# Soft-MoE and random-feature attention over 16 batch rows: paired clips and exponentials, a copy moved to ScalarE, two contexts moved to another PSUM bank

## The reference, cut to what matters

```python
qkv = x @ Wqkv + bqkv                        # 16 heads of 8
xn = x / norm(x)                             # q and k, per head
proj = einsum('bhtd,rhdm->rbhtm', xn, omega) # R = 2 nodes, M = 32 features
feat = exp(clip(proj * sqrt(2 s) - s, -20, 20)) * const
# causal linear attention: ctx = qf . cumsum(kf x v), den = qf . cumsum(kf)
out_ch = ctx / maximum(den, 1e-6)
...
logits = einsum('bsd,etd->bset', xn, se)     # 512 slots
dispatch = softmax(logits, axis=experts); slots = dispatch^T xn
h = gelu(slots @ w1); processed = h @ w2     # hidden 512
out = softmax(logits, over all slots) @ processed
```

## Time and profile before

| | |
|---|---|
| median of 3 runs | 474.83 (474.27 to 476.93) |
| the profiled execution | 474.87, its span 473.1 |
| mean granted TensorE clock | 0.977 |
| one inner row, from `shift` to `shift` | 27.04 and 27.18 in turn |
| busy: PE / DVE / ACT / POOL | 435.3 / 376.0 / 314.4 / 186.7 |
| clips (L747) / exponentials (L533), 128 each | 98.8 / 87.8 |
| the stack's copy (L794) x15 | 13.8 |

### The profile page before, as it was taken

The page is one execution under the profiler, slowest core; times in us unless marked ns, Lnnn a source line. Parts: engine busy times, 40 slices in busy tenths (PEclk is TensorE's granted clock), DMA queues, the critical chain, the costliest instruction groups (busy, mean ns, idle before and its releaser), DMA issues.

```text
span 473.1 us, 16005 instructions
## 1 busy us (share of the span) xinstructions
PE 435.3 (92%) x5712; PEld 359.2 (76%) x5712; DVE 376.0 (79%) x956; ACT 314.4 (66%) x577; POOL 186.7 (39%) x276
## 2 busy tenths in 40 slices
PE   3087999999999999999999999999999999999993
PEld 2056888888787888788887888878788887888782
DVE  5579788887988888887988889788898879677462
ACT  4226768676758667686766768675767767676761
POOL 4303444443533343353334345353334435334220
PEclk9589999999999999999999999999999999999998
DMA  2430202020020202011020202002020201102000
GB/s 54 99 65 1 46 13 48 24 46 21 12 51 11 53 13 44 24 32 24 11 55 11 44 22 44 17 6 55 11 50 17 44 11 24 34 2 58 1 13 12
DMA packets 45779, 14.46 MB, mean 31 GB/s; under 512 B 35640, under 2 KB 45624, under 8 KB 45752
## 3 DMA queue, kind: packets, MB, share of 16 engines
q1 hardware_dynamic: 45176, 13.77, 13.9%
q10 hardware_dynamic: 576, 0.33, 0.2%
HBM read 3.61 MB, written 2.10 MB: 12 GB/s over the span
## 4 chain that ended last, share of the span: by engine, by line
PE 68%; DVE 21%; issue 5%; SPq 2%; ACT 2%; DMA 1%; DVEq 1%
PE x L952 11%; PE p_s L1003 8%; PE x L1160 7%; PE x L1172 6%; PE p_t L1003 6%; DVE arg L747 6%; PE p_s L1015 5%; PE x L1151 4%; PE x L1015 3%; PE x L1094 3%; DVE slot_v L802 3%; PE p_s L988 2%; PE x L1129 2%; DVE s_sb L753 2%; PE x L1105 2%
## 5 line engine op out<-in xcount | busy, mean ns | idle before, releaser
L464 POOL TENSOR_TENSOR s_sb<-s_sb,causal 128x256 f32<-128x256 f32 x96 | 68.6, 734 | 112.3 <-ACT s_sb L538 110.3
L533 ACT ACTIVATE feat<-arg,f_bias 128x512 f32<-128x512 f32 x128 | 87.8, 717 | 0.2
L747 DVE TENSOR_SCALAR arg<-p_s,f_low,f_high 128x512 f32<-128x512 f32 x64 | 48.8, 803 | 13.4 <-PE p_s L988 13.4
L1003 PEld LDWEIGHTS p_s<-feat 64*64 64x64 f32 x1024 | 38.6, 132 | 18.2 <-issue 16.5
L311 POOL TENSOR_TENSOR qk_sq<-qkv 128x512 f32<-128x512 f32 x15 | 15.6, 1041 | 92.5 <-DVE qkv L724 92.5
L747 DVE TENSOR_SCALAR arg<-p_t,f_low,f_high 128x512 f32<-128x512 f32 x64 | 50.0, 801 | 0.0
L1003 PE MATMUL p_s<-feat 64*64 64x256 f32 (+3 forms) x1024 | 49.5, 309 | 0.0
L1003 PE MATMUL p_t<-feat 64*64 64x256 f32 (+3 forms) x1024 | 46.1, 296 | 0.0
L458 POOL TENSOR_TENSOR s_sb<-s_sb,causal 128x512 f32<-128x512 f32 x30 | 37.6, 1273 | 17.2 <-ACT s_sb L544 17.2
L1003 PEld LDWEIGHTS p_t<-feat 64*64 64x64 f32 x1024 | 41.5, 133 | 1.5
L1121 PEld LDWEIGHTS x<-xg,disp 128*128 128x128 f32 x256 | 29.8, 191 | 7.9 <-ACT disp L560 7.9
(11 more groups left out here) (155 smaller groups left out, 1021.7 us busy)
## 6 DMA issues: line engine op xcount, KB each, us to landing
out_dram<-out_sb SPq DMA_DIRECT2D x32, 64.0 KB, 2.1
xin<-in_L_attn_x_dram SPq DMA_DIRECT2D x31, 64.0 KB, 2.4
omega_f<-in_L_attn_omega_dram SPq DMA_DIRECT2D x16, 4.0 KB
se_rows<-n_L_ffn_slot_embeds_dram SPq DMA_DIRECT2D x1, 256.0 KB, 2.6
w_f<-in_L_ffn_w_dram SPq DMA_DIRECT2D x1, 256.0 KB, 3.6
w_sb<-in_L_ffn_w_dram SPq DMA_DIRECT2D x1, 256.0 KB, 3.6
stack_t<-stack SPq DMA_TRANSPOSE x16, 4.3
wqkv_f<-in_L_attn_Wqkv_dram SPq DMA_DIRECT2D x1, 192.0 KB, 4.1
```

The lines of the kernel that those rows point to most:

```text
L464: pool.tensor_tensor(v, v, m, ALU.mult).then_inc(mb_ok, 1)
L533: nc.scalar.activation(feat[:, p % 4, :], arg[:, p % 4, :], ACT.Exp, bias=f_bias[:, 0:1]).then_inc(fe_ok, 1)
L747: nc.vector.tensor_scalar(arg[:, p % 4, :], bank, f_low[:, 0:1], f_high[:, 0:1], ALU.max, ALU.min).then_inc(cl_ok, 1)
L1003: mm = nc.tensor.matmul(dst[rows:rows + 64, u, o:o + hi - lo], f[:, T + keys:T + keys + 64], f[:, lo:hi], start=True, stop=True, skip_grou ...
```

## The change

`clip` and `feature_exp` take a group g (two pairs, both halves of a bank pair: 128 x 1024) instead of a pair: four of each a row instead of eight. Two of the four merged ones come at other places of the lists. The stack's copy is made by ScalarE from `qk_n`, behind `evac_b(b, 3)`. Contexts 2 and 3 go to `x01[:, 1, 0:256]`, both token tiles into one bank, so `lump_high` waits for `slots_norm` (`slv_ok`) instead of `qkv_bias`; `hidden` waits for `ctx_copy` before its m = 1 and for `qkvs_ok` before its second half. `ln_apply` is split into `ln_newton`, which keeps its place, and `ln_scale`, which goes behind `evac_a` 2 and 3. `place_v` goes behind `mask_b` 2 and 3.

```diff
             def home(b, g):
+            if g == 1 and not is_row(b, B - 1):
+                return x01[:, 1, 0:256].rearrange("p (j t) -> p j t", j=TILES)
...
 # gpsimd row
                     stack_low(pool, b1)
-                    place_v(b1)
                 mask_b(b, 2)
                 mask_b(b, 3)
+                if nxt:
+                    place_v(b1)
...
+            def feature_exp(b, g):
+                after(act, cl_ok, count(b, 4, g + 1))
+                after(act, sb_ok, count(b, 8, 2 * g - 2))
+                k = 2 * g % 4
+                nc.scalar.activation(feat[:, k:k + 2, :], arg[:, k:k + 2, :], ACT.Exp,
+                                     bias=f_bias[:, 0:1]).then_inc(fe_ok, 1)
...
 # scalar row
                 feature_exp(b, 0)
-                feature_exp(b, 1)
...
                 slots_high(b)
-                feature_exp(b, 2)
-                feature_exp(b, 3)
                 evac_b(b, 0)
+                feature_exp(b, 1)
                 evac_b(b, 1)
...
                 evac_b(b, 3)
+                if nxt:
+                    nc.scalar.activation(stacked(2), parted(), ACT.Copy).then_inc(stcp_ok, 1)
                 nc.scalar.preload_act_table_set(LN_EXP)
                 proc_copy(b, 0)
-                feature_exp(b, 4)
+                feature_exp(b, 2)
                 proc_copy(b, 1)
                 if not first:
                     attn_copy(bp)
-                feature_exp(b, 5)
+                feature_exp(b, 3)
                 if nxt2:
                     xt_high(b2)
-                feature_exp(b, 6)
-                feature_exp(b, 7)
...
+            def clip(b, g):
+                after(dve, ft_ok, count(b, 4, g + 1))
+                after(dve, fg_ok, count(b, 4, g + 1))
+                after(dve, fe_ok, count(b, 4, g - 1))
+                k = 2 * g % 4
+                nc.vector.tensor_scalar(arg[:, k:k + 2, :], (p_s, p_t)[g % 2][:, :, :], f_low[:, 0:1], f_high[:, 0:1],
+                                        ALU.max, ALU.min).then_inc(cl_ok, 1)
...
 # vector row
                 clip(b, 0)
-                clip(b, 1)
-                clip(b, 2)
                 slots_norm(b, 0)
                 slots_norm(b, 1)
-                clip(b, 3)
+                clip(b, 1)
...
                 if nxt2:
-                    ln_apply(b2)
-                if nxt:
-                    stack_again(b1)
+                    ln_newton(b2)
                 evac_a(b, 2)
                 evac_a(b, 3)
+                if nxt2:
+                    ln_scale(b2)
                 if not first:
                     ctx_norm(bp)
-                clip(b, 4)
-                clip(b, 5)
-                clip(b, 6)
-                clip(b, 7)
+                clip(b, 2)
+                clip(b, 3)
...
 # lump_high
                     after(pe, mb_ok, count(b, 8, 8))
-                    if nxt:
-                        after(pe, qkvs_ok, count(b, 1, 3))
-                    else:
-                        after(pe, ec_ok, count(b, 1, 2))
+                    after(pe, slv_ok, count(b, 2, 4))
...
+            def hidden(b, first, nxt, half):
+                elif nxt:
+                    after(pe, qkvs_ok, count(b, 1, 2))
...
                 for m in (2 * half, 2 * half + 1):
+                    if m == 1 and not first:
+                        after(pe, cs_ok, count(b, 2, 0))
```

More of the change, by code:

```diff
@@ L293, in home @@
         def home(b, g):
+            if g == 1 and not is_row(b, B - 1):
+                return x01[:, 1, 0:256].rearrange("p (j t) -> p j t", j=TILES)
             if g == 1:
-                return x23
-            return x01 if is_row(b, B - 1) else p_s
+                return x23[:, :, 384:512]
+            return (x01 if is_row(b, B - 1) else p_s)[:, :, 384:512]
         def load_omega(eng, a):
@@ L548, in ctx_copy @@
                 after(act, ct_ok, count(b, 1, 0))
-                nc.scalar.activation(ctx_sb[:, g, :].rearrange("p (j t) -> p j t", j=TILES), home(b, g)[:, :, 384:512],
+                nc.scalar.activation(ctx_sb[:, g, :].rearrange("p (j t) -> p j t", j=TILES), home(b, g),
                                      ACT.Copy).then_inc(cs_ok, 1)
@@ L695, in ln_stats, with ln_newton @@
                 nc.vector.tensor_scalar(small[:, VE, 2:4], mv[:, :, 1], VAR_FLOOR, None, ALU.max).then_inc(ln_s, 1)
-            def ln_apply(b):
+            def ln_newton(b):
                 after(dve, ln_a, count(b, 2, 2))
@@ L700, in ln_apply, with ln_scale @@
                 newton(VE, VY, VT, 4, ln_n, b, 3)
+            def ln_scale(b):
                 after(dve, sl_ok, count(b, 2, -2))
@@ L790, in slot_maxima @@
                                             AX_X, ALU.max).then_inc(mx_ok, 1)
-            def stack_again(b):
-                after(dve, sthi_ok, count(b, 1, 1))
-                nc.vector.tensor_copy(stacked(2), stacked(0)).then_inc(stcp_ok, 1)
             def slots_norm(b, half):
@@ L830, in _ @@
             ln_stats(b0)
-            ln_apply(b0)
+            ln_newton(b0)
+            ln_scale(b0)
             dve.wait_ge(d_qkv, 16)
@@ L885, in _ @@
                                     ALU.subtract).then_inc(se_l, 1)
-            ln_apply(b1)
+            ln_newton(b1)
+            ln_scale(b1)
             def row(b, first, nxt, nxt2):
@@ L992, in scores @@
             def scores(b, p):
-                after(pe, fe_ok, count(b, 8, p + 1))
+                after(pe, fe_ok, count(b, 4, p // 2 + 1))
                 if p in (0, 1, 4, 5):
-                    hold(pe, cl_ok, count(b, 8, (2, 4, 0, 0, 6, 8)[p]))
+                    hold(pe, cl_ok, count(b, 4, (1, 2, 0, 0, 3, 4)[p]))
                 else:
@@ L1010, in context @@
                 dst = home(b, a // 2)
+                one_bank = a // 2 == 1 and not is_row(b, B - 1)
                 for kt, j in ((0, 0), (0, 1), (1, 1)):
@@ L1014, in context @@
                         o = 128 * (kt + j)
-                        mm = nc.tensor.matmul(dst[32 * q:32 * q + 32, j, 384:512], vw[:, b[1], kt, QUADS * a + q, :],
-                                              s_sb[:, p, q % 2, o:o + 128], start=(kt == 0 and a % 2 == 0),
+                        mm = nc.tensor.matmul(dst[32 * q:32 * q + 32, j, :], vw[:, b[1], kt, QUADS * a + q, :],
+                                              s_sb[:, p, q % 2, o:o + 128],
+                                              start=(kt == 0 and a % 2 == 0 and not (one_bank and j == 1)),
                                               stop=(kt == j and a % 2 == 1), skip_group_check=True)
@@ L1030, in lump_low, with lump_high @@
                 context(b, 1)
-            def lump_high(b, nxt, last):
+            def lump_high(b, last):
                 after(pe, ea_ok, count(b, 6, 6))
@@ L1130, in slots_transposed @@
                 mm.then_inc(slt_ok, 1)
-            def hidden(b, first, half):
+            def hidden(b, first, nxt, half):
                 if half == 0:
@@ L1135, in hidden @@
                     after(pe, slh_ok, count(b, 1, 1))
-                elif not first:
-                    after(pe, cs_ok, count(b, 2, 0))
+                elif nxt:
+                    after(pe, qkvs_ok, count(b, 1, 2))
                 else:
-                    pe.wait_ge(qkvs_ok, 2)
+                    after(pe, ec_ok, count(b, 1, 1))
                 for m in (2 * half, 2 * half + 1):
+                    if m == 1 and not first:
+                        after(pe, cs_ok, count(b, 2, 0))
                     sl = slice(128 * m, 128 * m + 128)
@@ L1219, in row @@
                 if not first:
-                    lump_high(bp, nxt, False)
+                    lump_high(bp, False)
                 if first:
@@ L1223, in row @@
                     pe.wait_ge(d_late, 16 * LATE)
-                hidden(b, first, 0)
-                hidden(b, first, 1)
+                hidden(b, first, nxt, 0)
+                hidden(b, first, nxt, 1)
                 scores(b, 2)
@@ L1248, in _ @@
             scores(last_row, 7)
-            lump_high(last_row, False, True)
+            lump_high(last_row, True)
             ctx_transposed(last_row)
```

## The result

The changed kernel takes 485.0 (484.45 to 485.87, 4 runs) against 475.0 (474.27 to 476.93, 4 runs) for the one before: a ratio of 1.0204, with an interval of 1.0183 to 1.0225. It is slower by about 2% (the interval lies on both sides of 1.02, and clear of 1), and the forecast of 483.7 was 1.3 short. The profiled execution took 484.45, with a span of 482.7 against 473.1, so 9.6 of span have to be found.

What follows compares the result with a forecast made beforehand. TensorE, busy for 92% of the span, was taken as the bound. Twelve rows losing 0.58 (7.0) plus 1.9 for rows 1, 14 and 15 gave +8.9 on 474.83: 483.7, range from 474.5 up to case C (493).

Steps and rivals of the forecast that it cites:

- The stall of 0.29: TensorE's wait for slot_v after qkv_product in a row: said to go whole, with 0.15 of it kept.
- The merged instructions: Price of one merged clip, 1.30, and one merged exponential, 1.15, which no row of the profile showed.
- The middle: Context transposes to combine: the stall at the projections goes, but proc_copy 1 behind the merged exponential stops combine instead.
- the third chunk: Part of combine that needs proc_copy 1: can start 4.05 after ctx_norm starts, at 241.86 in the forecast case.
- the sum: Whole kernel: 12 x 0.58 = 7.0 plus 1.9 for rows 1, 14 and 15, together +8.9; setup, row 0, tail unchanged.
- rival C: GpSimd masks slip in twice among the scales, also ahead of their one-element products: +18, 493; chance 0.16.
- A: No GpSimd mask slips in between VectorE's scales: 0.04 lost per row, +1.9, 476.8; chance 0.27.
- B: The forecast: one GpSimd mask slips in between VectorE's first and second scale, 0.58 lost per row; chance 0.40.
- the block: VectorE's scales wait while GpSimd's stack_low runs, to 236.51; ctx_norm starts at 237.27 instead of 237.17.
- second stall: TensorE's wait around projections 2 and 3, some 0.57 on average in 12 rows: said to go whole.

Runs made afterwards that it cites:

- the early w1: The changed kernel with row 0's split of w1 on VectorE put in front of token_maxima: 482.16, ratio 1.0137.
- the moved exponential: The changed kernel with ScalarE's merged exponential 2 moved behind proc_copy 1 and attn_copy: 466.40, ratio 0.9827.

## Why the prediction was right

**The head.** The stall of 0.29 went, and half of it was kept: `processed_low` starts at 234.63 on the old clock, and the prediction said 234.64. Its picture was right but for the place of the rest: about 0.1 of it lies in front of `processed_low`, behind gelu 0, which ends at 239.98, and about 0.1 at scores 0 and 1, which take 1.36 here (232.88 to 234.24) and 1.27 before, since scores 1 waits for the merged clip 1 (it ends at 233.39). Row 14 kept the same 0.15 (12.19 from `shift` to `processed_low` against 12.34).

**The merged instructions.** Exponential 1.147 (1.15 forecast); clip 1.336 (1.30), 0.04 short. Both were worked out from how other instructions of the same engine grow with their length, and that held.

**The middle.** `ctx_norm` starts at 237.64 on the old clock (237.81 forecast) and the third chunk at 241.68 (241.86): 4.04 after it, where 4.05 was summed. The forecast is 0.17 late by the scales. A scale that is blocked ends only 0.09 and 0.08 after the GpSimd instruction it waited for (242.01 behind 241.92, 242.75 behind 242.67), not 0.21 and 0.14 as the sum had it: most of its own time seems to be spent by then. So both scales take 0.82 here, not about 1.1 and 0.9, and `combine` stops for 1.08 (245.10 + 0.90 to 247.08), not 1.2. That one mask slips in and no second one is what the timeline shows; the two products of one column run at 0.26 beside the next mask, as they do elsewhere, so rival C's condition doesn't hold. The mask decided between A and B: the runs with the block or only the mask taken away give 477.49 and 478.38, where 476.8 was forecast for A. The Trainium skill, "SBUF — State Buffer", section "SBUF: two separate sides", describes this as a lock that is held for a whole instruction; the 820 against 340 of the scales agree with it.

**The size of a row.** Forecast +0.58, measured +0.51. The third chunk came 0.18 earlier than forecast, which alone makes +0.40. The missing 0.11 lie behind it: after a stop the last eight matmuls of `combine` take 1.00 (247.08 to 248.08, and the same in every row from 1 to 15), where half of the sixteen was put at 0.90. The sum took the third chunk's start as the end of the loss, and a restart costs something as well. Row 1 and row 14, with the same chain and no second stall to win, give +1.05 and +0.59 (0.96 and 0.46 forecast); row 14 by the same restart.

**What the sum left out.** Setup and row 0 were put at nothing and are +1.74. Two parts. Up to the first `shift` it is +0.58, but the ten experiments, which leave the setup alone (but for the early w1), spread there from 32.91 to 33.88 in one execution each, so that this can't be laid to the change. In row 0 it is +1.16: the wait for the second part of w1 grew from 2.46 to 2.82, `hidden` lost 1.32 at the lower clock, and the rest of the row gave some back. Row 15 and the end are +0.08 instead of +0.46. The row itself is as forecast: -0.28 up to the context transposes (its head stall, 1.16 before and 0.72 now, was larger than in the other rows) and +0.73 in `combine`, +0.45 together. But the four last matmuls of the kernel took 0.71 in this execution and 1.09 in that of the kernel before. That is the clock: over them the granted clock was 1.00 here and 0.58 there. In the twelve profiled executions they took 0.71 or 0.72 five times, at 0.90 to 1.00, and 1.06 to 1.22 seven times, at 0.50 to 0.60. The seven are of both kinds of kernel, the five all have the change; why the clock fell earlier in some isn't shown.

So three errors in the sum (the row 0.07 a time too long, rows 0 and setup missing, the end too high) partly cancelled. The distance of 1.3 to the median is luck in part; the mechanism, its place and its size per row are what was right. Which of B (0.40) and A (0.27) came hung on one alternation of two engines that no row of the kernel before showed in that place, so to land on B rather than A was partly luck too.

**What isn't settled.** Ahead of `hidden` in row 0 the same 2.82 of idle time led to the lower clock in the profiled executions of four kernels (the changed one, the one with the scales back and the two with split exponentials) and not in those of three others (the moved exponential, `place_v` back and contexts back). What decides it is left open here. In the five kernels with less idle time there (2.46 or 1.03) the clock was 1.00. By the times: the early w1 gives 2.84 on the changed kernel (485.0 to 482.16), and row 0 alone gave 1.70 where the clock hadn't fallen (27.15 to 25.45), so most executions of the changed kernel probably had it. This was only argued.

## What to carry to other kernels

A merged instruction saves work only on its own engine, which is worth nothing where another engine sets the pace (12.3 on VectorE here), and it delays its first half and all that is queued behind it: ask what stands behind it on an engine that works in order, and put the copy that the bottleneck waits for ahead of it. When a stall is taken away, walk each engine's list from that point to the next thing the bottleneck needs, since the slack that the stall gave to that chain goes with it. Where VectorE and GpSimd work on SBUF side by side, order both lists together: an edit that changed only what GpSimd had next was worth 0.43 a row here.

## What the runs showed of the hardware

Several VectorE instructions from SBUF to SBUF stood still while a GpSimd instruction ran, and ended shortly behind it. How shortly differs. The scales (128 x 128, 0.34 free) ended 0.08 to 0.09 after it, the maximum in `qk_norms` (128 x 64, 0.195 free) about 0.05. A newton step of 128 x 4, which takes 0.16 free, took 1.03 and ended 0.01 to 0.02 after it; these are VectorE's and GpSimd's timelines of the changed kernel:

```profile
238.63 1.03 DVE L680 SCALAR_TENSOR_TENSOR small<-small 128x4 f32<-128x4 f32 x1 [0.21 <-DVE small L684]
```

```profile
238.57 1.08 POOL L318 TENSOR_TENSOR qk_n<-qkv,small 128x512 f32<-128x512 f32 x1 [1.55 <-DVE small L684]
```

Between two scales GpSimd's next instruction got in. Not every such instruction is held, so the prediction's sentence on this was too wide. The scales' products of one column (128 x 1) took 0.26 beside GpSimd. The sum of the squares (L735, 128 x 512 to 128 x 64) took 0.67 to 0.69 whether the masks ran beside it (rows 1 to 15) or not. BATCH_NORM_STATS2 (L690, 128 x 128) took 0.27 to 0.30 everywhere.

TensorE paid about 0.1 for a stop in the middle of a run of small matmuls, beside the stop itself (1.00 instead of 0.90 for eight). And behind an idle time of 2.82 on TensorE in row 0 the granted clock was 0.50 in four of seven profiled executions; behind one of 2.46 or 1.03 it was 1.00 in all five.
